# Where the query's lower half is computed: one DVE subtraction from PSUM in place of an ACT copy and a POOL subtraction

## The reference

```python
x = x + tanh(g_xattn) * attention(layernorm(x), ctx)      # 16 heads of 32, softmax, then Wo
x = x + tanh(g_ffn)   * ffn(layernorm(x))
# attention: Q = xn @ Wq.T ; K, V = ctx @ Wk.T, ctx @ Wv.T ; softmax(Q K^T / sqrt(32)) V @ Wo.T
# ffn: xr, xk = mixes of each token with the one before it, by mu_r and mu_k
#      sigmoid(xr @ W_r.T) * ((relu(xk @ W_k.T) ** 2) @ W_v.T)
```

## Time and profile before

| what | value |
|---|---|
| median of 3 runs | 1597.43 us (1596.37 to 1598.52) |
| the profiled execution | 1598.47 us |
| its span, first to last instruction | 1596.8 us |
| mean granted TensorE clock | 0.958 |
| busy: PE, DVE, ACT, POOL | 1425.5 (89%), 1083.4 (68%), 777.7 (49%), 702.5 us (44%) |
| chain that ended last, by engine | PE 54%, DVE 12%, issue 11%, POOL 10%, ACT 10% |

### The profile page before, as it was taken

The page is one execution under the profiler, slowest core; times in us unless marked ns, Lnnn a source line. Parts: engine busy times, 40 slices in busy tenths (PEclk is TensorE's granted clock), DMA queues, the critical chain, the costliest instruction groups (busy, mean ns, idle before and its releaser), DMA issues.

```text
span 1596.8 us, 28336 instructions
## 1 busy us (share of the span) xinstructions
PE 1425.5 (89%) x9616; PEld 1037.8 (65%) x9616; DVE 1083.4 (68%) x1862; ACT 777.7 (49%) x1412; POOL 702.5 (44%) x871
## 2 busy tenths in 40 slices
PE   7866899998989899898989989898989989898978
PEld 7734666676666667566666767666666756666656
DVE  3465766767777676777677676777667677776662
ACT  3345364554637364554636455463735545463531
POOL 1111454536354553535355353634545363544444
PEclk9978899999999999999999999999999999999989
DMA  5422011121201012120201112120111212020100
GB/s 166 124 86 73 21 47 40 53 59 46 65 26 59 26 53 58 46 65 26 70 26 61 39 53 59 46 59 32 46 39 53 59 46 65 26 63 22 44 24 33
DMA packets 98364, 84.09 MB, mean 53 GB/s; under 512 B 49440, under 2 KB 62752, under 8 KB 98336
## 3 DMA queue, kind: packets, MB, share of 16 engines
q1 hardware_dynamic: 98336, 83.72, 17.5%
HBM read 58.79 MB, written 20.71 MB: 50 GB/s over the span
## 4 chain that ended last, share of the span: by engine, by line
PE 54%; DVE 12%; issue 11%; POOL 10%; ACT 10%; DMA 1%; SPq 1%; ACTq 0%; DVEq 0%; POOLq 0%
PE g_bank L1010 30%; PE g_bank L1184 5%; PE o_bank L1139 4%; ACT buf L512 4%; DVE mm L833 3%; PE s_bank L1089 3%; ACT pq L612 3%; POOL buf L425 3%; ACT s_bank L613 3%; PE d_bank L1145 3%; DVE place L887 3%; PE s_bank L1113 2%; DVE buf L742 2%; POOL rstd L406 2%; PE s_bank L1010 2%
## 5 line engine op out<-in xcount | busy, mean ns | idle before, releaser
L837 DVE TENSOR_TENSOR pq<-s_bank,pq 128x512 f16<-128x512 f32 x320 | 218.8, 687 | 115.4 <-ACT s_bank L613 115.1
L1184 PE MATMUL g_bank<-buf,WkT 128*128 128x512 f32 x768 | 226.0, 442 | 69.6 <-DVE buf L742 69.2
L833 DVE TENSOR_REDUCE mm<-s_bank 128x3 f32<-128x462 f32 (+1 forms) x384 | 201.0, 576 | 127.0 <-PE s_bank L1089 126.9
L512 ACT ACTIVATE buf<-place 128x512 fp32r<-128x512 f32 x208 | 127.4, 628 | 222.4 <-DVE place L887 123.4
L1184 PEld LDWEIGHTS g_bank<-buf,WkT 128*128 128x128 f32 x768 | 155.5, 212 | 116.3 <-DVE buf L742 67.5
L612 ACT ACTIVATE pq<-s_bank 128x512 f16<-128x512 f32 x320 | 191.1, 597 | 56.5 <-PE s_bank L1117 56.5
L1010 PE MATMUL g_bank<-WrT,buf 128*128 128x512 f32 x768 | 192.5, 400 | 17.9 <-POOL buf L425 15.3
L1010 PE MATMUL g_bank<-xnT,WqT 128*128 128x512 f32 x768 | 202.1, 406 | 3.6 <-DVE xnT L821 2.1
L445 POOL TENSOR_TENSOR buf<-place,buf 128x512 fp32r<-128x512 f32 x64 | 82.6, 1291 | 264.3 <-ACT buf L512 264.3
L613 ACT ACTIVATE s_bank<-s_bank 128x512 f32<-128x512 f32 x320 | 193.7, 605 | 0.0
L1010 PE MATMUL g_bank<-WvT,buf 128*128 128x512 f32 x768 | 190.7, 394 | 0.0
(11 more groups left out here) (127 smaller groups left out, 2240.2 us busy)
## 6 DMA issues: line engine op xcount, KB each, us to landing
xa<-in_x SPq DMA_DIRECT2D x64, 256.0 KB, 2.7
x<-in_x SPq DMA_DIRECT2D x64, 256.0 KB, 2.7
out<-x SPq DMA_DIRECT2D x48, 256.0 KB, 2.0
k_all<-k_scratch SPq DMA_DIRECT2D x16, 256.0 KB, 2.9
k_low<-k_scratch SPq DMA_DIRECT2D x16, 256.0 KB, 3.0
v_main<-v_scratch SPq DMA_DIRECT2D x16, 256.0 KB, 2.8
place<-x SPq DMA_DIRECT2D x16, 256.0 KB, 2.3
out<-place SPq DMA_DIRECT2D x16, 256.0 KB, 2.0
```

What stands on the lines that cost most here:

```text
L512: nc.scalar.activation(dst, src, ACT.Copy).then_inc(done, 1)
L833: nc.vector.reduce_max(maxima, scores, AX.X).then_inc(reduced, 1)
L837: nc.vector.tensor_tensor(pq[:, n, LO, :], score_bank[5 * g + n][:, :], pq[:, n, HI, :], ALU.subtract).then_inc(p_lo, 1)
L1184: ins = nc.tensor.matmul(K_BANK[c][:, :], WkT2[:, s, e, cols(c)], buf3[:, m, e, :], start=(e, n) == (0, 0), stop=(e, n) == (C - 1, len(PRO ...
```

## The change

The ACT copy and POOL's subtraction go. DVE gets `q_low`, of the same form as `xT_low`. All waits on `q_copied` become waits on `q_lo`, which DVE now raises. The tile `q32`, the two waits for it (`xT_done` or `q_lo` on ACT, `q_lo` in `mix_k(2)` on DVE) go with it. Everything else keeps its order.

```diff
@@ POOL @@
-            def q_low(i, g):
-                pool.wait_ge(q_copied, i * G + g + 1)
-                nc.gpsimd.tensor_tensor(buf4[:, LO, g, :], q32[g], buf4[:, HI, g, :].bitcast(F32), ALU.subtract).then_inc(q_lo, 1)
...
             for t in range(TT):
                 norm(0, 0, t)
-            for g in range(G):
-                q_low(0, g)
...
                 attn_low(i, G - 1)
-                if pre:
-                    q_low(i + 1, 0)
-                    q_low(i + 1, 1)
                 for t in range(TT):
                     norm(1, i, t)
-                if pre:
-                    q_low(i + 1, 2)
                 first_column(i)
...
                     mix_low(i, buf3, c, xk32, xk_hi, xk_lo)
-                if pre:
-                    q_low(i + 1, 3)
                 if ffn:
                     output(i - 1, TT - 1)
@@ ACT @@
-            def q_split(i, g, loop):
+            def q_high(i, g, loop):
                 act.wait_ge(q_done, i * G + g + 1)
                 if loop:
                     act.wait_ge(scores_done, i * SCORE_UNITS)
                 high(buf4[:, HI, g, :], Q_BANK[loop][g][:, :], q_hi)
-                if g < 2:
-                    act.wait_ge(xT_done, i * TT + g + 3)
-                else:
-                    act.wait_ge(q_lo, i * G + g - 1)
-                nc.scalar.activation(q32[g], Q_BANK[loop][g][:, :], ACT.Copy).then_inc(q_copied, 1)
@@ DVE @@
+            def q_low(i, g, loop):
+                dve.wait_ge(q_hi, i * G + g + 1)
+                low(buf4[:, LO, g, :], Q_BANK[loop][g][:, :], buf4[:, HI, g, :], q_lo)
@@ DVE, prologue @@
             for t in range(TT):
                 xT_low(0, t)
-            for r in range(4):
-                reduce_max(0, r)
+            q_low(0, 0, False)
+            q_low(0, 1, False)
+            reduce_max(0, 0)
+            q_low(0, 2, False)
+            reduce_max(0, 1)
+            q_low(0, 3, False)
+            reduce_max(0, 2)
+            reduce_max(0, 3)
@@ DVE, step @@
                 if pre:
+                    q_low(i + 1, 0, True)
                     reduce_max(i + 1, 0)
+                    q_low(i + 1, 1, True)
                     reduce_max(i + 1, 1, (0, 1))
...
                 if pre:
+                    q_low(i + 1, 2, True)
                     reduce_max(i + 1, 2)
...
                 mix_k(i, 3, pre)
+                if pre:
+                    q_low(i + 1, 3, True)
                 xk_low(i, 3)
                 keep_carry(i)
@@ PE, query @@
                 if not loop:
-                    later(pe, q_copied, g - 1)
+                    later(pe, q_lo, g - 1)
@@ PE, project @@
                 elif pre:
-                    pe.wait_ge(q_copied, (i + 1) * G + t + 1)
+                    pe.wait_ge(q_lo, (i + 1) * G + t + 1)
@@ PE, ffn_k @@
                 elif c == 1 and queries:
-                    pe.wait_ge(q_copied, (i + 1) * G + 4)
+                    pe.wait_ge(q_lo, (i + 1) * G + 4)
```

More of the change, by code:

```diff
@@ L102, in flamingo_block @@
         xn2 = (xa[:, 0, :], xa[:, 1, :])
-        q32 = (xa[:, 2, :], xa[:, 3, :], xa[:, 2, :], xa[:, 3, :])
         diff = (th[0], attn32, xa[:, 0, :], xa[:, 1, :])
@@ L140, in flamingo_block @@
         xT_done, xT_hi, xT_lo = sem("xT_done"), sem("xT_hi"), sem("xT_lo")
-        q_done, q_hi, q_copied, q_lo = sem("q_done"), sem("q_hi"), sem("q_copied"), sem("q_lo")
+        q_done, q_hi, q_lo = sem("q_done"), sem("q_hi"), sem("q_lo")
         max_done = sem("max_done")
@@ L654, in _ @@
             for g in range(G):
-                q_split(0, g, False)
+                q_high(0, g, False)
             def step(i, ffn, pre):
@@ L707, in step @@
                 if pre:
-                    q_split(i + 1, 0, True)
-                    q_split(i + 1, 1, True)
+                    q_high(i + 1, 0, True)
+                    q_high(i + 1, 1, True)
                 norm2(i, 0, pre)
@@ L717, in step @@
                 if pre:
-                    q_split(i + 1, 2, True)
+                    q_high(i + 1, 2, True)
                 x2_copy(i, 3)
@@ L722, in step @@
                 if pre:
-                    q_split(i + 1, 3, True)
+                    q_high(i + 1, 3, True)
                 xk_high(i, 2)
@@ L884, in mix_k @@
                     later(dve, k2_lo, i * C)
-                elif c == 2 and pre:
-                    dve.wait_ge(q_lo, (i + 1) * G + 3)
                 nc.vector.scalar_tensor_tensor(xk32[c], diff[c], mu[:, 1, c:c + 1], x2[:, c, 0:N], ALU.mult, ALU.add).then_inc(xk_mixed, 1)
@@ L1028, in weights_transposed @@
                     if EARLY_UNITS <= u < EARLY_UNITS + 2:
-                        pe.wait_ge(q_copied, G)
+                        pe.wait_ge(q_lo, G)
                     elif u >= 2:
@@ L1308, in step @@
                         beside(1)
-                    pe.wait_ge(q_copied, (i + 1) * G + 3)
+                    pe.wait_ge(q_lo, (i + 1) * G + 3)
                     query(i + 1, 3, True, at(1, lambda: maxima(i + 1, 3)))
```

## The result

| | before | after |
|---|---|---|
| median (lowest to highest), 10 runs each | 1598.36 us (1596.37 to 1601.05) | 1603.49 us (1599.22 to 1607.2) |
| profiled execution, its span | 1598.47, 1596.8 | 1601.19, 1599.5 |
| mean granted clock | 0.958 | 0.956 |
| busy PE, DVE, ACT, POOL | 1425.5, 1083.4, 777.7, 702.5 | 1427.3, 1107.7, 747.8, 613.4 |
| first restart (join 0) | 188.60 | 198.50 |

The ratio is 1.0034 [1.002, 1.0047]: the changed kernel is slower by 0.34%. The two profiled executions are 2.7 us apart: +9.9 up to the first restart, -7.9 in the steps, +0.7 behind them. In the medians 5.1 us lie between the kernels. Both parts that the prediction set against each other are there. In this one execution the loss up to the first restart is near the forecast (9.9, for 10.8) and the gain in the steps is smaller (7.9, for 11.4); the medians lie further apart than the two executions do.

What follows compares the result with a forecast made beforehand. PE bounds the kernel, busy 1425.5 of 1596.8 us. Prologue +10.8, joins -9.0 and pauses -2.4 make -0.6, so 1598.47 becomes 1597.9 in the profiled execution, 1.04 above the median: 1596.8 us forecast, range 1591 to 1603.

Steps and rivals of the forecast that it cites:

- Part 1: In the steps: removed ACT copies count nothing; without POOL's q_low(2), PE restarts 0.16 us earlier per join, 2.4 us gained.
- Part 2: In 14 joins, all but join 0: PE gains from DVE's earlier round 4 reduction, 9.0 us in all.
- Part 4: Prologue: q_low ahead of reductions makes each stage a serial loop of 6.47 us; costs 10.8 us, between 9.3 and 12.3.
- Both ends of the term: Joins: gain of 6.2 us with each join's clock unchanged, 12.6 if all have the short low clock.
- rival B: Joins: slower, long low clock in most, so DVE's earlier reductions buy nothing; 1603.2 us, chance 0.13.
- The drift: Joins: long and short low-clock stretches come in runs that drift with step length; shorter steps give another pattern.
- the 0.75 that the prediction named as a sign: Steps: each should become shorter by 0.75 us on average if the forecast is right.
- The claim on `keep_carry`: Joins: with POOL's output finished earlier, DVE's four-column copy takes 0.16 us, not 1.24.
- Part 3: Steps: q_low added to DVE, 0.681 us each and 41 us in all, fits idle gaps; counted at nothing.
- C: Prologue: faster, the 10.8 us delay is caught up if step 0 waited for late weights' loads; 1586 us, chance 0.07.
- D: Joins: slower, the carry copy stays at 1.24 us through another cause, only 2.4 gained; 1605.8 us, chance 0.05.
- A: Joins: faster, short low clock in nearly all of them; 1593.2 us, chance 0.20.

Runs made afterwards that it cites:

- after_again: The changed kernel unedited, measured and traced again on the same chip as the follow-up kernels: 1604.40 us, 1.0033 of the kernel before.
- prologue_only: The kernel before with only the changed kernel's DVE prologue order for block 0; later queries as before: 1610.24 us, ratio 1.0074.
- order: The changed kernel with each reduction in DVE's prologue put ahead of the q_low that needs a later query: 1590.17 us, 0.995 of the kernel before.
- order_fill: The order kernel plus 12 matmuls with unused results in PE's pause ahead of each join: 1581.60 us, 0.9893 of the kernel before.
- order_act: The order kernel plus an ACT copy of 128x512 from SBUF to an unread tile behind each query's HI: 1587.75 us, 0.9927 of the kernel before.
- before_fill: The kernel before plus 12 matmuls with unused results at the end of each step: 1603.96 us, ratio 1.0041.

## Why the prediction was wrong

It said 1596.8 us and no measurable change; it is 1603.49 and slower by 0.34%. The mechanisms were right. What failed are sizes: the gain in the steps (Parts 1 and 2), the low clock behind the prologue's pauses (Part 4), and the step from one execution to the median. Against the measured median all three err to the same side.

**The sum, term by term.** For the profiled execution the sum said 1597.9, and 1601.19 came, 3.3 more: the first restart was 9.9 us late and not 10.8 (-0.9), the steps gained 7.9 and not 11.4 (+3.5), and the stretch behind them was 0.7 longer. Then the prediction took 1.04 off to reach the median, as in the kernel before. The changed kernel's median is 2.3 above its profiled execution instead (4.3 in `after_again`): another 3.3 us. That the prologue's restarts vary from run to run, as the next paragraph has it, is likely a part of this; no run shows all of it.

**Part 4, the prologue, 10.8: right in one trace, too small in the median.** Rounds 0 to 4 took 11.1 us more in the first trace, 13.3 in that of `after_again` and 14.8 in that of `prologue_only`. In the medians the order costs 14.2 us in the changed kernel and 11.4 in the one before. The 9.3 at full clock hold: 6.44 and 6.43 us a stage were measured with the clock kept up, for 6.47. The step that failed is the price of a restart at the low clock. The upper end, 12.3, was for two restarts with four or five slow matmuls each, 1.4 us apiece. In `after_again` nearly the whole query runs slow: the twelve matmuls behind round 1 take 4.49 us at a mean clock of 0.65 and the nine behind round 2 take 4.21 at 0.50, where `order` has 3.06 and 2.33 at 1.00. The stage behind round 2 takes 8.66 us, so a restart costs up to 2.2. The stretch from round 4 to the first restart differs from trace to trace too, 98.6 to 104.8 us over the thirteen traces, with 31 to 42 us of it at the low clock. What of the medians' 14.2 lies there I have not taken apart.

**Part 2, the joins, 9.0: 7.3** in the profiled execution (95.27 - 87.94), 6.6 in `after_again`. Both ends of the term hold. DVE lets round 5 start even earlier than the 5.8 forecast: at 5.65 in `order_fill`. The value between the ends was a guess at how many joins stay long: 9.0 means fewer than four of 14, and five were (six in `after_again`). No row of before could settle it, since in eight of its joins DVE's lateness hid how long PE itself would take. The 5.9 us that the upper end and rival B take for a short join was an estimate of mine, and no run shows it as one figure: in joins 3 to 6 and 10 to 12 of before PE needs 5.69 to 5.95 us without the wait, 2.91 to 3.41 of them at 0.50 (join 9 has 6.19 at 0.50), and the short joins after took 5.79 to 5.88. The drift shows in the traces: in joins 3 to 6 of before, 91.55 to 91.60 us apart, the low clock begins 0.50 us ahead of the restart, then 0.11, 0.67 and 1.26 behind it; after, where two short joins in a row are 90.5 to 90.6 us apart, it moves by 1.5 to 1.7 us between them.

**Part 1, the pause, 2.4: about 1.4, and 0.8 of it lost again.** PE's pause fell by 0.14 to 0.17 us as forecast, but the stretch from round 5 to the next restart fell only by 0.10, from 84.85 to 84.74; 13 such steps make 1.4; why not the whole 0.16 of each I have not found out. The stretch behind join 14 was 0.5 longer than before's, and join 0 and the stretch behind it 0.3. So the steps gained 7.3 + 1.4 - 0.8 = 7.9 us, not 11.4: 0.53 a step, for the 0.75 that the prediction named as a sign. The claim on `keep_carry` was right to the digit: 0.16 us in every join.

**Parts 1 and 3, counted at nothing:** right. The row of DVE's subtractions from `g_bank`, 64 of its 72 being `q_low`, has a mean of 0.688 us; `xT_low` had 0.681. ACT's 64 copies put back as others cost nothing. DVE is busy 1107.7 us, 1115 was forecast.

**Rivals.** B, slower through long stretches of the low clock in most joins, gave 1603.2, close to the time that came, but for another reason: five joins of 14 were long, not ten, and the joins gained more than the 5.2 from which B decides. What it had right is that the low clock takes back part of the gain. Not every pause was followed by the low clock. In the prologue after, round 1 takes 0.93 us at 0.50 behind a pause of 2.92, but round 2 takes 0.57 at 1.00 behind one of 2.90. In the steps after, each of joins 1 to 14 has its stretch of low clock, begun at most 1.2 us behind the restart that ends a pause of 3.91; the filled ones of `order_fill`, behind a pause of 1.21, are at 1.00 throughout. C falls: of the 11.1 us that rounds 0 to 4 took longer, 9.9 are there at the first restart. Nor was there a wait for loads that could have hidden them: between round 4 and the first restart PE has one wait for a DMA, 3.03 us long, for 3.71 before. D falls with the copy at 0.16. A, short stretches nearly everywhere, did not come about by itself; `order_act`, with 11 short joins of 14, comes nearest.

**The execution and the median.** The steps were added up for one execution, and the same kernel's runs lie up to 8 us apart (1599.22 to 1607.2), as wide as the effects that were to be told apart. Of the miss of 6.7 us in the median, 0.9 is the kernel before itself, which now measured 1598.36 and not 1597.43. By the medians of the experiments the rest is the prologue, 3.4 too small (14.2 for 10.8), and what the change gains elsewhere, 2.7 too large (8.7 for 11.4); measured on another chip, these come to 6.1 for the 5.8 that are left. So which part failed most depends on the measure: the gain in the steps by the trace, the prologue by the medians.

## What to carry to other kernels

When an instruction moves to another engine's queue, read what each place in that queue waits for: a 0.69 us subtraction put one place ahead of a reduction turned a pipelined prologue into a serial loop and cost more than the 8.7 us that the change gains elsewhere. A small DVE instruction that reads and writes SBUF can last until the POOL instruction beside it ends (here 1.24 us, for 0.16), so look at who runs beside it and not only at its size. And where PE pauses in each pass, count the slow matmuls behind the pause as a cost of the pause: matmuls of no use in it were worth 8.6 us in a kernel whose other engines were in time, and lost 5.1 in one where they were not.

## What the runs showed of the hardware that was not expected

- The share of long stretches of low clock went with small changes in the length of a step: 84.65 us from round 5 to the restart gave 3 long joins of 14, 84.74 gave 5, 84.92 gave 8. The medians moved by -2.4 and +7.9 us. These are one profiled execution each, and `after_again` has 6 long joins where `after`, the same kernel, has 5, so this is seen and not shown.
- A pause of 1.21 us with one of 0.60 behind it was followed by no low clock in any join (`order_fill`). Pauses of 1.34 and 1.69 were followed by the low clock in 6 of 14 steps (`before_fill`). Between its two pauses each kernel has one more, of 0.32 to 0.35 us.
- The row of a DVE instruction that is held by POOL calls it busy: 1.23 to 1.25 us for a copy of 128x4 that takes 0.16 by itself.
